# Summing the expert rows into the residual during the expert phase of a cross-attention and mixture-of-experts layer

## The chip, the cores and the metric

The kernel runs as one program on one core of a Trainium2 chip. The metric is the device time of one execution in microseconds (us); lower is better. An execution is somewhat longer than the span of the profile, which goes from the first instruction to the last.

## What is computed

64 sequences of 128 tokens with 256 features pass through one layer in float32. Cut to what matters:

```python
ln = layernorm(x)                                  # 64 x 128 x 256
x  = x + cross_attention(ctx, ln, mask, ...)       # 4 heads of 64, keys from ctx and from x itself
h  = layernorm(x)
w, idx = route(h)                                  # 4 of 32 experts for each token, with weights
mixed  = sum over the 4 of  w * down_e( silu(gate_e(h)) * up_e(h) )
shared = shared_down( silu(shared_gate(h)) * shared_up(h) )
x  = x + mixed + shared
```

So the output row of a token is its residual row, plus four weighted rows from four experts, plus one row from the shared expert.

## The kernel before

The order of all work is written out by hand, with semaphores between the engines. A unit is two sequences (256 tokens); there are 32. A tile is 128 rows that all go to one expert; there are 287 (`TILES`). The program has three stages.

**Attention, 32 units.** For each unit the engines project, score, mix and route. The residual of all 64 sequences stays in SBUF (`x1`). `rows_to_scatter` (L1099) normalises the new residual, `turn_n1` (L742) turns it on TensorE so that the features lie on the partitions, and `n1_copy` (ACT, L1188) copies the turned rows into the tile `n1T`, from which the router's logits are computed. For the first `EARLY` = 8 units SyncE also saves `n1T` to the DRAM tensor `n1T_kept` (`save_n1T`, L407), and `n1_copy` of the next unit waits until that has landed. For all units VectorE keeps the mean and the scale of each row in `mr` (L1446, L1447), at the end of the chain that makes them. GpSimd scatters four copies of each normalised row into the DRAM tensor `lists`, sorted by expert (`scatter_row`, L556); SyncE makes the copies (`spread_rows`, L401) and blanks the pages (L389). SyncE's queue is in order: what waits there holds back all behind it.

At the end of this stage the shared expert of the first 8 units is computed (`shared_up` L916, `shared_down` L927), while the last rows are still scattered, from turned rows that `load_n1T` (L417) has loaded back.

**Expert phase, 287 tiles.** SyncE loads tile t (`load_tile`, L466) into one of 8 slots (`xs`, parts of `pay`), as soon as TensorE has turned tile t - 8. In its iteration t TensorE projects tile t (L1033), turns tile t + 2 (L1024), and multiplies tile t - 1 by its expert's down weights (L1043). ACT evicts and applies silu (L1315, L1320, L1326). VectorE's iteration t is, in this order: `hidden(t)` (L1865), `keep_dest(t + 4)` (L1878), which reads the last two columns of tile t + 4, and `weigh_result(t - 1)` (L1872). GpSimd scatters the weighted rows into the DRAM tensor `expert_out` (L701), where the four rows of a token lie side by side. The rows of unit u can be in any tile up to tile 39 + 8u, and in no later one.

**Last stage, units 8 to 31.** After the last tile, ACT normalises the residual of a unit again from `mr` (`norm_again`, L1272), TensorE turns it (`shared_turn`, L895), ACT copies it to SBUF (`turned`, L1279), and TensorE computes the shared expert (L916, L927). VectorE multiplies (L1747), adds the shared result to `x1` (L1755), and sums the four expert rows of a unit (`sum_experts`, L1895 and L1897) and the residual (`sum_all`, L1903; `sum_last`, L1910) into `res`. SyncE loads the four rows of a unit (`load_er`, L484, 1 MB) and stores the sums (`store`, L488; the last unit in two halves, L498). Because the first 8 units have no shared work left, 32 units are summed within the time of 24.

## Time and profile before

| | us |
|---|---|
| median of 3 runs | 1342.62 |
| lowest and highest | 1340.92, 1345.98 |
| the profiled execution's own time | 1343.46 |
| its span | 1341.5 |
| attention stage, with the early shared work, in the span | 0 to about 742 |
| expert phase | about 742 to 1193 |
| last stage | 1193 to 1341.5 |

The profile's tables name an engine, a line of the kernel and the tiles written and read. PE is TensorE's matmul, PEld its weight load, DVE VectorE, ACT ScalarE, POOL GpSimd, SP SyncE with the queue SPq. A matmul in float32 shows as two records in the trace, so the 8 matmuls of a `shared_up` half (2 of the gate, 2 of the up weights, each two records) read as x8. The engines' busy shares of the span are TensorE 97%, ACT 75%, VectorE 72% and GpSimd 48%; they are means over three stages that have different limits.

### The profile page before, as it was taken

The numbers are of one execution on the slowest core, as the hardware profiler recorded it, in microseconds if no ns is written. First come the engines' busy times: TensorE is split into PE (matmuls) and PEld (weight loads), VectorE is DVE, ScalarE is ACT, GpSimd is POOL, SyncE is SP. The second block draws the span as 40 slices with busy tenths as digits, with TensorE's granted clock in tenths as the row PEclk, the third lists the DMA queues.
The fourth block names the chain that finished last, engine by engine and source line by source line (L and its number), as shares of the span: only waits on it lengthen the run. The fifth ranks groups of instructions, "written<-read, shape, count | busy, mean of one in ns | idle before, by whom it ended". The sixth has DMA issues, their size and how long they took to land.

```text
span 1341.5 us, 32944 instructions
## 1 busy us (share of the span) xinstructions
PE 1298.0 (97%) x8718; PEld 1043.2 (78%) x8718; DVE 972.0 (72%) x4498; ACT 1011.6 (75%) x2730; POOL 643.4 (48%) x724
## 2 busy tenths in 40 slices
PE   6999999999999999999979899999999999999997
PEld 4566676676676766766658799999999999988886
DVE  4578898888988988888887455555555555548887
ACT  4899999999999999999851566766776676653332
POOL 1113555555555555555455366666666666640000
PEclk8999999999999999999989899999999999999999
DMA  8234645535545445454487655555655555438896
GB/s 278 84 133 136 205 162 176 192 131 187 176 138 190 161 153 195 136 179 162 168 304 246 194 169 172 172 172 168 178 169 174 169 173 166 132 114 313 304 319 218
DMA packets 147714, 247.14 MB, mean 184 GB/s; under 512 B 24139, under 2 KB 110413, under 8 KB 146896
## 3 DMA queue, kind: packets, MB, share of 16 engines
q1 hardware_dynamic: 121472, 177.63, 41.3%
q0 software_dynamic: 26064, 67.42, 14.5%
q8 instruction: 77, 1.26, 0.4%
q14 instruction: 101, 0.83, 0.2%
HBM read 104.68 MB, written 119.96 MB: 167 GB/s over the span
## 4 chain that ended last, share of the span: by engine, by line
PE 63%; ACT 21%; DVE 9%; issue 5%; DMA 2%; SPq 0%; POOL 0%; ACTq 0%; DVEq 0%
PE psT L1033 10%; PE ps L1033 9%; PE psS L1043 9%; ACT arena L1168 6%; PE ps L916 6%; PE ps L1024 5%; PE ps L852 4%; ACT arena L1160 4%; PE psS L927 3%; PE psT L827 3%; PE psS L813 3%; PE psO L840 2%; ACT arena L1128 2%; ACT arena L1132 2%; ACT arena L1175 2%
## 5 line engine op out<-in xcount | busy, mean ns | idle before, releaser
L701 POOL DMA_INDIRECT expert_out<-pay,dest x287 | 282.1, 983 | 175.1 <-DVE dest L1878 157.4
L556 POOL DMA_INDIRECT lists<-pay,slot x168 | 174.3, 1037 | 187.7 <-PE psT L827 39.6
L1043 PE MATMUL psS<-arena,history 128*128 x574 | 171.8, 381 | 0.3 <-DVE history L1865 0.3
L1033 PEld LDWEIGHTS ps<-pad,hist_j 128*128 128x128 f32 x1152 | 152.1, 193 | 9.5 <-ACT pad L1315 2.1
L1033 PEld LDWEIGHTS psT<-pad 128*128 128x128 f32 x1144 | 151.0, 192 | 7.3
L1033 PE MATMUL ps<-pad,hist_j 128*128 128x128 f32 x1152 | 152.8, 276 | 1.9 <-ACT pad L1315 1.9
L1033 PE MATMUL psT<-pad 128*128 128x128 f32 x1144 | 151.6, 276 | 0.0
L1872 DVE TENSOR_SCALAR pay<-psS,dest 128x256 f32<-128x256 f32 x287 | 138.9, 484 | 1.6 <-PE psS L1043 1.5
L757 PE MATMUL ps<-arena 128*128 128x512 f32 x256 | 128.3, 624 | 2.6 <-ACT arena L1120 2.0
L556 POOL DMA_INDIRECT lists<-arena,slot x88 | 91.0, 1034 | 79.4 <-PE psT L827 20.6
L1168 ACT ACTIVATE arena<-arena,rden 128x256 f32<-128x256 f32 x256 | 109.1, 503 | 15.2 <-DVE rden L1466 15.1
L1865 DVE TENSOR_TENSOR history<-history,psT 128x128 f32<-128x128 f32 x143 | 41.2, 288 | 102.4 <-ACT history L1326 102.4
L1865 DVE TENSOR_TENSOR history<-history,ps 128x128 f32<-128x128 f32 x144 | 41.5, 288 | 101.2 <-ACT history L1326 101.2
L1024 PE MATMUL ps<-ident,pay 128*128 128x128 f32 x574 | 110.0, 274 | 3.1 <-DMA arena<-in_gate_up 3.0
L1315 ACT ACTIVATE pad<-ps 128x256 f32<-128x256 f32 x287 | 107.7, 375 | 0.0
L1320 ACT ACTIVATE hist_j<-arena 128x512 f32 x144 | 89.6, 622 | 9.4 <-issue 7.6
L1326 ACT ACTIVATE history<-ps 128x128 f32<-128x128 f32 x144 | 39.9, 277 | 70.3 <-PE ps L1033 70.3
L757 PEld LDWEIGHTS ps<-arena 128*128 128x128 f32 x256 | 44.2, 193 | 59.2 <-issue 59.2
L1320 ACT ACTIVATE pad<-arena 128x512 f32 x143 | 88.8, 621 | 0.0
L1326 ACT ACTIVATE history<-psT 128x128 f32<-128x128 f32 x143 | 39.7, 278 | 65.0 <-PE psT L1033 65.0
L1043 PEld LDWEIGHTS psS<-arena,history 128*128 128x128 f32 x574 | 86.9, 192 | 0.7 <-issue 0.7
L1418 DVE TENSOR_REDUCE va<-arena 128x12 f32<-128x768 f32 x64 | 61.0, 953 | 34.2 <-ACT arena L1128 29.1
(238 smaller groups left out, 3284.1 us busy)
## 6 DMA issues: line engine op xcount, KB each, us to landing
lists<-pad SPq DMA_DIRECT2D x72, 516.0 KB, 5.2
pay<-lists SPq DMA_DIRECT2D x287, 129.0 KB, 2.2
arena<-expert_out SPq DMA_DIRECT2D x32, 1024.0 KB, 7.1
pay<-pay SPq DMA_DIRECT2D x42, 384.0 KB, 3.6
x<-in_x SPq DMA_DIRECT2D x32, 256.0 KB, 4.7
out<-arena SPq DMA_DIRECT2D x31, 256.0 KB, 5.8
arena<-arena SPq DMA_DIRECT2D x20, 384.0 KB, 3.4
arena<-in_ctx SPq DMA_DIRECT2D x32, 192.0 KB, 4.6
```

The lines of the kernel that those rows point to most:

```text
L556: pool.indirect_dma_start(lists, bass.IndirectOffsetOnAxis(ap=slots(u)[:, j, k:k + 1], axis=0), paid(u)[:, j, k, :], None).then_inc(scat[3 ...
L701: pool.indirect_dma_start(expert_out, bass.IndirectOffsetOnAxis(ap=dest[:, t % DESTS, 1:2], axis=0), yy[n], None, bounds_check=T * TOPK - ...
L757: m = pe.matmul(ps[0][:, :], lnT[:, k, tok], w_lat[:, k, 0:2 * D], start=k == 0, stop=k == 1)
L916: m = pe.matmul(up_banks[u % 2][mm][:, which * D:(which + 1) * D], w[:, k, mm * P:(mm + 1) * P], n1T_of(u)[:, k, :], start=k == 0, stop=k ...
L1024: m = pe.transpose(ps[n % 2][:, k * P:(k + 1) * P], xs[n][:, k * P:(k + 1) * P], ident[:, :])
L1033: m = pe.matmul(ps[2 + n % 2][:, which * P:(which + 1) * P], w_now[1 - n % 2][:, k, which * I:(which + 1) * I], xsT[:, n % 2, k * P:(k + 1 ...
L1043: pe.matmul(dbank[n % 2][:, 0:D], hh[:, n % 4, :], w_dn[:, at(e, 1), :].rearrange("p a n -> p (a n)"), start=True, stop=True)\
L1168: a = act.activation(probs[:, j, g, :], probs[:, j, g, :], ACT.Copy, scale=rden[:, j, g:g + 1])
L1315: act.activation(xsT[:, n % 2, :], ps[n % 2][:, 0:D], ACT.Copy).then_inc(xst_ev, 1)
L1320: act.activation(w_now[1 - n % 2], w_gu[:, at(e, 1)].rearrange("p a k n -> p (a k) n"), ACT.Copy)\
L1865: dve.tensor_tensor(hh[:, n % 4, :], sg[:, n % 4, :], ps[2 + n % 2][:, P:2 * P], ALU.mult)\
L1872: dve.tensor_scalar(yy[n], dbank[n % 2][:, 0:D], dest[:, t % DESTS, 0:1].bitcast(fp32), None, ALU.mult)\
```

## The change

Five things are changed together.

1. The four expert rows of units 0 to 28 (`IN_PHASE` = 29) are summed into `x1` in the expert phase. SyncE loads them in pieces of two rows for each token of one sequence (`load_piece`, 256 KB, 116 pieces) into a new tile `side` with room for 3 pieces, one piece after every second tile from tile 55 on. Each piece waits until the piece three before it has been added. The first piece of unit u also waits until all tiles up to 39 + 8u are scattered. VectorE adds one row of a piece (`add_row`, 128 x 256) at the end of each of its iterations 53 to 284, 232 in all.
2. Units 0 to 7 are stored to the output in the expert phase, the others in the last stage, straight from `x1`. `res` and `sum_all` are gone. Units 29, 30 and 31 are still summed in the last stage, from loads of 1 MB.
3. The turned rows of all 32 units are saved to `n1T_kept`, and `n1_copy` waits for the save before it at every unit.
4. `norm_again`, `shared_turn`, `turned` and `mr` are gone. The last stage loads the turned rows of units 8 to 31 from DRAM: unit 8 into `side`, the others into a ring of four (`n1T_ring`).
5. TensorE waits, ahead of the last stage, for the last tile's turned rows and hidden rows, no longer for the last weighted result; that wait is now ahead of the first `shared_down` of the stage.

The masks and the bias of the output projection now share SBUF with `side`, since they are last read before the first piece arrives.

```diff
+PIECES = 3
+IN_PHASE = 29
+PIECE_LOAD, PIECE_ADD = 55, 53
+N1T_RING = 4
...
-                if (s + -2).exists() and s.n - 2 < EARLY:
+                if (s + -2).exists():
                     save_n1T(s + -2)
...
             spread_rows(Unit(UNITS // 2 - 1, 0))
-
+            save_n1T(Unit(UNITS // 2 - 1, 0))
...
+            def load_piece(q):
+                u, b, half = q // 4, q // 2, q % 2
+                if q % 4 == 0:
+                    for n in range(SLOTS):
+                        sp.wait_ge(y_out[n], 16 * (E // SLOTS + 1 + u))
+                ge(sp, summed, 2 * (q - PIECES + 1))
+                sp.dma_start(side[:, q % PIECES, :].rearrange("p (k n) -> p k n", k=2), er_d[:, b, 2 * half:2 * half + 2, :])\
+                  .then_inc(piece_in[q % PIECES], 16)
...
             for t in range(TILES):
                 load_tile(t, t % SLOTS)
...
+                q, odd = divmod(t - PIECE_LOAD, 2)
+                if odd == 0 and 0 <= q < 4 * IN_PHASE:
+                    load_piece(q)
+                done, odd = divmod(t - PIECE_LOAD - 17, 8)
+                if odd == 0 and 0 <= done < EARLY:
+                    sp.wait_ge(summed, 8 * (done + 1))
+                    store(done)
...
+            sp.wait_ge(summed, 2 * 4 * IN_PHASE)
+            sp.dma_start(side[:, 0, :], n1T_kept[EARLY]).then_inc(first_n1T_in, 16)
+            sp.wait_ge(w_ready, TILES)
+            for u in range(EARLY + 1, EARLY + 1 + N1T_RING):
+                load_late_n1T(u)
             for n in range(SLOTS):
                 sp.wait_ge(y_out[n], 16 * ((TILES - 1 - n) // SLOTS + 1))
...
+            for u in range(EARLY, UNITS - 1):
+                sp.wait_ge(sx_done, 2 * u + 2)
+                if u + N1T_RING + 1 < UNITS:
+                    load_late_n1T(u + N1T_RING + 1)
+                store(u)
...
-            pe.wait_ge(yy_done, TILES)
-            shared_turn(EARLY)
+            pe.wait_ge(xst_ev, TILES)
+            pe.wait_ge(hh_done, TILES)
             for u in range(EARLY, UNITS + 1):
                 if u < UNITS:
                     shared_up(u, 0)
-                if u + 1 < UNITS:
-                    shared_turn(u + 1)
-                if u < UNITS:
                     shared_up(u, 1)
                 if u >= EARLY + 1:
                     shared_down(u - 1)
...
-                ge(act, n1T_saved, 16 * upto(u.n, EARLY))
+                ge(act, n1T_saved, 16 * u.n)
...
-                    dve.scalar_tensor_tensor(mr[:, at(2 * u.n, 2), 0], mv[:, 4:6, 0], -1.0, ra[:, 4:6], ALU.mult, ALU.mult)
-                    dve.tensor_copy(mr[:, at(2 * u.n, 2), 1:2], ra[:, 4:6].rearrange("p (j o) -> p j o", o=1))
...
+            def add_row(q, k):
+                dve.wait_ge(piece_in[q % PIECES], 16 * (q // PIECES + 1))
+                ge(dve, summed, 2 * q + k)
+                xb = x1[:, q // 2, :]
+                dve.tensor_tensor(xb, xb, side[:, q % PIECES, k * D:(k + 1) * D], ALU.add).then_inc(summed, 1)
...
                 if t >= 1:
                     weigh_result(t - 1, (t - 1) % SLOTS)
+                if 0 <= t - PIECE_ADD < 2 * 4 * IN_PHASE:
+                    add_row((t - PIECE_ADD) // 2, (t - PIECE_ADD) % 2)
```

Three places show how the order moves. The changed kernel has other line numbers: its L1859, L1872, L1866 are L1865, L1878, L1872 before; its L469 is L466; its L936 and L949 are L916 and L927.

VectorE in the expert phase, two tiles, before (`history` holds the hidden rows, `pay` the tile slots and results, `dest` the kept columns):

```order
L1865 TENSOR_TENSOR history<-history,ps 128x128
L1878 COPY dest<-pay 128x2
L1872 TENSOR_SCALAR pay<-psS,dest 128x256
L1865 TENSOR_TENSOR history<-history,psT 128x128
L1878 COPY dest<-pay 128x2
L1872 TENSOR_SCALAR pay<-psS,dest 128x256
```

The same two tiles after the change:

```order
L1859 TENSOR_TENSOR history<-history,ps 128x128
L1872 COPY dest<-pay 128x2
L1866 TENSOR_SCALAR pay<-psS,dest 128x256
L1879 TENSOR_TENSOR x<-x,side 128x256
L1859 TENSOR_TENSOR history<-history,psT 128x128
L1872 COPY dest<-pay 128x2
L1866 TENSOR_SCALAR pay<-psS,dest 128x256
L1879 TENSOR_TENSOR x<-x,side 128x256
```

One add stands behind each weighted result, and ahead of the next tile's hidden rows.

SyncE's queue in the expert phase, with what each transfer waits for; before, the tile loads stand alone between the last weights and the loads of the last stage:

```order
L466 DMA pay<-lists 128x258 x6
L466 DMA pay<-lists 128x258 [waits dest_kept,xst_full] x279
L484 DMA arena<-expert_out 128x2x1024 [waits y_out5,y_out4,y_out6,y_out3,y_out7,y_out2,dn_full,y_out1,y_out0]
L484 DMA arena<-expert_out 128x2x1024 x3
L484 DMA arena<-expert_out 128x2x1024 [waits dC]
```

After the change, one unit's share of the queue:

```order
L481 DMA side<-expert_out 128x512 [waits y_out5,y_out4,y_out6,y_out3,y_out7,y_out2,summed,y_out1,y_out0]
L469 DMA pay<-lists 128x258 [waits dest_kept,xst_full]
L485 DMA out<-x 128x2x256 [waits summed]
L469 DMA pay<-lists 128x258 [waits dest_kept,xst_full]
L481 DMA side<-expert_out 128x512 [waits summed]
L469 DMA pay<-lists 128x258 [waits dest_kept,xst_full] x2
L481 DMA side<-expert_out 128x512 [waits summed]
```

Every second tile load now stands behind a piece that waits for VectorE's adds (`summed`).

TensorE in the last stage, one unit and the start of the next, before:

```order
L916 MATMUL ps<-arena,w_sg 128x256 x2
L916 MATMUL ps<-arena,w_su 128x256 x2
L895 MATMUL psO<-ident,arena 128x128 x4
L916 MATMUL ps<-arena,w_sg 128x256 x2
L916 MATMUL ps<-arena,w_su 128x256 x2
L927 MATMUL psS<-w_sd,arena 128x256 x4
L916 MATMUL psT<-arena,w_sg 128x256 x2
```

After:

```order
L936 MATMUL ps<-arena,w_sg 128x256 x2
L936 MATMUL ps<-arena,w_su 128x256 x2
L936 MATMUL ps<-arena,w_sg 128x256 x2
L936 MATMUL ps<-arena,w_su 128x256 x2
L949 MATMUL psS<-w_sd,arena 128x256 x4
L936 MATMUL psT<-arena,w_sg 128x256 x2
```

The four transposes between the halves of a unit are gone; the rest keeps its order.

## Rows read from the trace of the kernel before

**Rows 1.** Windows: PE, PEld, DVE, ACT, POOL busy us; granted clock; DMA share; GB/s.
```profile
760.00:1190.00 430.00, 430.00 (x3345) 415.68 (x3344) 231.69 (x835) 299.83 (x837) 273.61 (x280) 1.00 0.56 163
1196.00:1200.00 4.00, 4.00 (x14) 3.19 (x14) 0.30 (x1) 1.11 (x3) 0.16 (x1) 0.57 0.34 76
1204.00:1330.00 126.00, 126.00 (x628) 111.00 (x627) 105.35 (x177) 48.61 (x110) 0.00 (x0) 1.00 0.89 311
```

**Rows 2.** Chain that ended last, one unit of the last stage (start, us, what).
```profile
1303.81 1.73 PE psT L916 x8
1305.54 0.44 PE psO L895 x4
...
1307.70 1.73 PE psS L927 x8
1309.43 1.73 PE ps L916 x8
```

**Rows 3.** The same chain, early shared work of the first units.
```profile
718.22 3.45 PE ps L916 x16
...
723.40 1.73 PE psT L916 x8
```

**Rows 4.** Timeline of TensorE at the head of the last stage.
```profile
1192.52 0.69 PE L1043 MATMUL psS<-arena,history 128*128 x2 [0.35 <-DVE history L1865]
...
1195.81 1.74 PE L916 MATMUL ps<-arena,w_sg 128*128 128x256 f32 x4 [0.69 <-ACT arena L1279]
...
1202.40 1.13 PE L916 MATMUL psT<-arena,w_sg 128*128 128x256 f32 x4 [0.75 <-ACT arena L1279]
```

**Rows 5.** Timeline of VectorE, two iterations before the end of the expert phase.
```profile
1189.56 0.48 DVE L1872 TENSOR_SCALAR pay<-psS,dest 128x256 f32<-128x256 f32 x1
```

**Rows 6.** DMA issues: size of each, median us from issue to landing.
```profile
pay<-lists SPq DMA_DIRECT2D x287, 129.0 KB, 2.2
out<-arena SPq DMA_DIRECT2D x31, 256.0 KB, 5.8
n1T_kept<-arena SPq DMA_DIRECT2D x8, 256.0 KB, 5.0
arena<-in_gate_up SPq DMA_DIRECT2D x1, 256.0 KB, 2.8
```

**Rows 7.** Timeline at the end of the program.
```profile
1329.58 1.89 PE L927 MATMUL psS<-w_sd,arena 128*128 128x256 f32 x8
...
1338.36 0.75 DVE L1910 TENSOR_TENSOR arena<-arena,x 128x256 f32<-128x256 f32 x2
```

**Rows 8.** Timeline of one tile in the middle of the expert phase.
```profile
961.32 0.98 POOL L701 DMA_INDIRECT expert_out<-pay,dest  x1 [0.56 <-DVE dest L1878]
...
962.06 0.60 PE L1043 MATMUL psS<-arena,history 128*128 x2
...
962.35 0.29 DVE L1865 TENSOR_TENSOR history<-history,psT 128x128 f32<-128x128 f32 x1 [0.71 <-ACT history L1326]
```

**Rows 9.** Timeline in the attention stage, VectorE and GpSimd side by side.
```profile
458.56 1.83 DVE L1454 TENSOR_TENSOR arena<-arena,ra 128x768 f32<-128x768 f32 x2
...
459.76 1.46 POOL L556 DMA_INDIRECT lists<-arena,slot  x1 [2.20 <-PE psT L827]
```

**Rows 10.** Timeline of GpSimd behind the last tile.
```profile
1195.18 0.98 POOL L701 DMA_INDIRECT expert_out<-pay,dest  x1 [0.30 <-issue]
```

**Rows 11.** Chain that ended last, the same step of attention in units 6 and 16 apart.
```profile
108.33 1.09 PE psT L827 x8
...
231.91 1.09 PE psT L827 x8
...
561.30 1.09 PE psT L827 x8
```

**Rows 12.** Timeline at the end of attention: SyncE's last copies, ACT's last turned rows.
```profile
691.62 1.29 SPq L401 DMA_DIRECT2D pay<-pay  x2
...
698.75 0.60 ACT L1188 ACTIVATE arena<-psO 128x512 f32<-128x512 f32 x1 [0.75 <-PE psO L742]
```

More of the change, by code:

```diff
@@ L342, in wide @@
             return v.rearrange("(a n) -> a n", a=1).to_broadcast([P, v.shape[0]])
-        er = arena[:, 0:ER_DEPTH * 2 * TOPK * D].rearrange("p (a j k n) -> p a j k n", a=ER_DEPTH, j=2, k=TOPK)
-        used[0] = ER_DEPTH * 2 * TOPK * D
+        er = arena[:, 0:(UNITS - IN_PHASE) * 2 * TOPK * D].rearrange("p (a j k n) -> p a j k n", a=UNITS - IN_PHASE, j=2, k=TOPK)
+        used[0] = (UNITS - IN_PHASE) * 2 * TOPK * D
         esum, e2 = part(2, D), part(2, 2, D)
-        res = part(2, 2, D)
-        late_set = [part(2 * D) for _ in range(4)]
+        late_set = [part(2 * D) for _ in range(2)]
+        n1T_ring = [part(2 * D) for _ in range(N1T_RING)]
+        assert used[0] <= E * 2 * D
         first_n1T, above, below_wo = 6, 6 + EARLY, 17
@@ L466, in load_tile, with store @@
                 sp.dma_start(xs[n], lists[at(t * P, P), :]).then_inc(xs_in[n], 16)
+            er_d = expert_out.rearrange("(b p k) n -> p b k n", p=P, k=TOPK)
+            out_d = out.rearrange("b p n -> p b n")
+            def load_piece(q):
[6 more added lines that the diff above has]
+                  .then_inc(piece_in[q % PIECES], 16)
+            def store(u):
+                sp.dma_start(out_d[:, 2 * u:2 * u + 2, :], x1[:, 2 * u:2 * u + 2, :]).then_inc(stored, 16)
+            sp.wait_ge(mask_ready, UNITS)
+            sp.wait_ge(biased, UNITS)
+            sp.wait_ge(s_full, NB)
             for t in range(TILES):
@@ L490, in _ @@
-            for v in range(ER_DEPTH):
-                load_er(v)
-            for v in range(UNITS - 1):
-                if v + ER_DEPTH < UNITS:
-                    load_er(v + ER_DEPTH)
-                store(v)
+            for v in range(IN_PHASE, UNITS):
+                sp.dma_start(er[:, v - IN_PHASE], er_d[:, 2 * v:2 * v + 2]).then_inc(er_in[v - IN_PHASE], 16)
+            for u in range(EARLY, UNITS - 1):
[3 more added lines that the diff above has]
+                store(u)
@@ L923, in shared_down @@
                     pe.wait_ge(pt_ev, NB - 1)
+                if u == EARLY:
+                    pe.wait_ge(yy_done, TILES)
                 for j in range(2):
@@ L1265, in _ @@
             in_order(step, UNITS)
-            def norm_again(u):
-                ge(act, nt_full, u - EARLY)
-                for j in range(2):
-                    b = 2 * u + j
-                    a = act.activation(n1_of(u)[:, j, :], x1[:, b, :], ACT.Identity,
-                                       bias=mr[:, b, 0:1], scale=mr[:, b, 1:2])
-                a.then_inc(nh, 1)
-            def turned(u):
-                act.wait_ge(nt_full, u - EARLY + 1)
-                ge(act, sgu_full, 2 * u)
-                act.activation(n1T_of(u).rearrange("p k n -> p (k n)"), psO[:, :], ACT.Copy).then_inc(nt_ev, 1)
             def shared_silu(u, mm):
@@ L1918, in _ @@
                     add_shared(u - 1)
[L1919 to L1923 removed]
+                if u % 3 == 1 and u // 3 - 5 in range(UNITS - IN_PHASE):
+                    sum_experts(IN_PHASE + u // 3 - 5)
+            dve.wait_ge(er_done, UNITS - IN_PHASE)
             add_shared(UNITS - 1)
[L1925 to L1926 removed]
 def kernel(x, ctx_768, mask_BxS2_bk0, L0_xattn_ln_x_g, L0_xattn_ln_x_b, L0_xattn_ln_l_g, L0_xattn_ln_l_b,
```

105 lines of the change are left out of this document (35 added, 70 removed).

## The prediction

> **What bounds the kernel now.** I read the windows of the span first, to see which stage has room, then the chain that ended last in each stage, then the timelines where stages meet, and the DMA issues last. In the expert phase TensorE is busy in all of the window at a granted clock of 1.00, while VectorE is busy 231.69 of 430 us, and the DMA engines 0.56 [rows 1]. In the body of the last stage TensorE is again busy throughout, and the DMA engines are at 0.89 with 311 GB/s, near the end of their range. So both stages are TensorE's, and a change gains only where it takes TensorE's work, or a gap of TensorE, away.
>
> The chain of the last stage has TensorE alone in it: a half of the shared up-projection 1.73 us, four transposes 0.44, the other half, the down-projection 1.73. Unit to unit it is 1309.43 - 1303.81 = 5.62 us [rows 2]. The early shared work has the same matmuls without the transposes, from loaded turned rows: 723.40 - 718.22 = 5.18 us a unit [rows 3]. This is what the changed last stage should look like, on the same chip in the same execution.
>
> **The change part by part, against the profiled execution (span 1341.5, own time 1343.46).**
>
> *Body of the last stage.* From the start of unit 9's up-projection on, 22 turns (units 10 to 31) are removed: 22 x 0.44 = 9.7 us [rows 2]. VectorE loses three large sums for each of 32 units, and has only hidden rows and shared adds left, with three units' sums among them; ACT loses three evictions a unit. Both were faster than TensorE there, so this gives nothing by itself. SyncE's loads fall from 32 MB to about 9 MB. A load of turned rows is issued when unit u's shared result is added, for unit u + 5, some three units (15 us) ahead of its use; a 256 KB transfer behind a 1 MB one took 5.8 us in the worst such company [rows 6]. It is covered.
>
> *Head of the last stage.* TensorE's last matmul of the tiles ends at 1192.52 + 0.69 = 1193.21. Then come the last weighted result, a normalisation, a turn and a copy, and the first up-projection starts at 1195.81, and unit 9's at 1202.40 [rows 4]: 9.2 us for what is 2 x 1.73 of matmuls. Behind the idle stretch the granted clock was 0.57, that is partly the lower of its two levels (1.2 instead of 2.4 GHz) [rows 1], and the first four matmul records took 1.74 us for 0.86. After the change unit 8's turned rows are loaded when the last add is done, in iteration 284: the weighted result of that iteration starts at 1189.56 [rows 5], the add ends some 0.8 us later, and a 256 KB load lands in 2.8 us [rows 6]: 1193.3. TensorE then idles for 0.1 to 0.5 us; I take 0.3. New head: 0.3 + 3.46 = 3.8 us, gain 5.4. Bounds: with a landing of 5.0 us [rows 6] the gap is 2.4 and the clock falls again, and the gain is 9.2 - 2.4 - 3.46 - 1.5 = 1.8 us; with no gap it is 5.7.
>
> *Tail.* The down-projection of unit 30 starts at 1329.58, and the program ends at 1341.5, 11.9 us later; VectorE's sums and a wait for a store lie between. The last add ends at 1338.36 + 0.75 = 1339.11, so the last store takes 2.4 us [rows 7]. After the change: two down-projections (3.46), one shared add of 0.42 with its wait (0.5), the store (2.4): 6.4 us, gain 5.5. Nothing in it is unknown, so its bounds are 5 and 6.
>
> *Expert phase, VectorE.* 232 adds of 128 x 256 from two SBUF inputs. Two such took 0.75 us together [rows 7], so one is about 0.37. VectorE idles 0.71 us ahead of each hidden row, waiting for ACT [rows 8], and that is exactly where the add stands; 0.34 remains. If it were late: the hidden row ends at 962.64, and the down-projection that needs it starts one tile (1.545 us, which is 430 us over 278 tiles) after 962.06, at 963.60 [rows 8]: another 0.96 us of slack. Cost 0. If both covers were gone, all 232 x 0.37 = 86 us would show, an end far from these rows.
>
> *Expert phase, GpSimd.* Its scatter takes 0.98 us, and the smallest gap between two was 0.30 [rows 8, 10]: a pitch of 1.28 for 1.545. In attention a scatter that began while VectorE ran an operation with two SBUF inputs took 1.46 us instead, and the VectorE operation was not longer [rows 9]. The add is of this kind. So a scatter may take up to 0.37 more: a pitch of 1.65, 0.1 over the tile. But then the scatter slides later against the add, meets less of it, and settles at the tile's pace; results have 8 slots. I take 0, the nearest end; the other is 232 x 0.1 = 23 us. The Trainium skill (SBUF — State Buffer, Who interferes with whom) says that a VectorE operation with two SBUF inputs contends with a GpSimd operation that reads SBUF, but infers that descriptor generation needs the other interface and is spared. By that inference the scatters would stay at 0.98 and this term is 0 for certain; the row of 1.46 speaks against it, and the sum is the same by both.
>
> *Expert phase, SyncE.* The piece that goes out after tile 55 + 2q waits for VectorE's iteration 48 + 2q, and tile 56 + 2q is behind it. VectorE needs that tile's last columns in iteration 52 + 2q. That is four iterations (6.2 us) less the 0.95 or so between the place of those columns in an iteration and its end: 5.2 us, of which 0.5 goes for the two issues. The tile load may take 4.7 us. It took 2.2 [rows 6]; with 256 KB ahead of it, at 311 GB/s [rows 1] 0.8 us, I take 3.0 to 3.4. The upper bound is 5.8, the stores behind 1 MB at a share of 0.89 [rows 6]. The new traffic is 116 pieces and 8 stores, 32 MB in 360 us or 90 GB/s, which at the last stage's rate (311 / 0.89) is 0.26 of the engines: 0.56 becomes 0.82. I take the lower, since a burst is 0.5 MB, not 1.3. Cost 0; what a miss costs is a rival.
>
> *Attention.* 24 more saves of 256 KB, each in SyncE's queue ahead of the next unit's loads, and a wait on ACT. Units with saves (to unit 7) took (231.91 - 108.33) / 6 = 20.60 us, those without (561.30 - 231.91) / 16 = 20.59 [rows 11]: nothing. Two small VectorE operations a unit leave, off the chain. The one tight place is the end: the save of unit 30 is issued at about 692.9, behind two copies, and ACT's last turned rows want it at 698.75 [rows 12], 5.8 us for a median of 5.0 [rows 6]. 0 to 2 us, and 0 is nearer.
>
> Sum: 9.7 + 5.4 + 5.5 = 20.6 us, less 0.4 for what the small margins may cost: the span becomes 1321.3, the execution (2.0 more) 1323.3. The profiled execution was 0.8 above the median, so the time is **1322 us**.
>
> **Rivals.**
>
> *The tile loads come late (slower).* The wait on the adds cuts SyncE's lead from eight tiles to about five. If a tile load takes L, four iterations cannot be shorter than 0.95 + 0.5 + L. It costs from L = 4.7 on, and at L = 5.1 a tile is 0.09 us longer, 232 of which eat the 20.6 us. At 5.8 a tile takes 1.81 and the program 20.6 - 61 = 41 us more than before: about 1383. For it: one in-order queue, and a share of 0.82. Against: 2.2 us now. Chance 0.08.
>
> *GpSimd becomes the pace.* If every scatter met a whole add in spite of sliding, 23 us would be lost and the time is about 1345, no change. The rows of 1.46 are for it, the sliding against. The same rule of the Trainium skill says that whichever of the two starts first holds the port and the other waits for all of it. As a mechanism here: an add that meets a running scatter waits up to 0.7 us, till 962.30, and the hidden row starts 0.3 late, inside its 0.96 of slack; the time would be 1322 again. With both, no change: chance 0.07.
>
> *A part of the gain is lost.* The head gets 1.8 instead of 5.4, or bursts on the full DMA engines cost half a microsecond in every tenth tile, or the last save stalls ACT by 2: 1326 to 1334. Chance 0.1.
>
> **How the numbers follow.** The forecast (1318 to 1326) has 0.75. A measurement can tell 0.5%, 6.7 us, from no change. Faster by more than that: the forecast and nearly all of the partial case, 0.84; the same: 0.08; slower: 0.08. The range reaches from 1317, where no gap and no stall is left, into the partial case at 1331.
>
> **What would show it.** Right: TensorE's chain of the last stage with 5.18 us a unit and no psO group; the first up-projection within 0.5 us of the last tile's down-projection, at full clock; the program's end some 6.4 us after unit 30's down-projection starts; the pitch of 1.545 us a tile unchanged, with VectorE's idle time ahead of the hidden row halved. Wrong: waits of VectorE on `pay<-lists` or on `side<-expert_out` in the expert phase; scatters of over 1.2 us with TensorE waiting on `yy_done`; a window of the expert phase in which TensorE is not at its full busy time; an ACT wait on `n1T_kept`.

## The result, and the profile after

| | before | after |
|---|---|---|
| median of the runs beside each other, us | 1343.59 (4 runs) | 1324.42 (4 runs) |
| lowest and highest | 1340.92, 1345.98 | 1321.65, 1327.15 |
| ratio, 95% interval | | 0.9858, 0.9829 to 0.9887 |
| the profiled execution's own time | 1343.46 | 1323.8 |
| its span | 1341.5 | 1321.7 |

The change takes 19 us off, 1.4%. The forecast was 1322 us in a range of 1317 to 1331. The profiled span is 19.8 us shorter, and three stretches make it up. Lines of the changed kernel: `shared_up` is L936, `shared_down` L949, the down-projection of the tiles L1065, the scatter L728, the new add L1879, the last columns' copy L1872.

Windows of the changed kernel, columns as in [rows 1]:

```profile
760.00:1190.00 430.00, 429.87 (x3343) 415.30 (x3341) 307.26 (x1065) 299.31 (x835) 319.62 (x278) 1.00 0.78 239
1200.00:1315.00 115.00, 115.00 (x534) 101.26 (x533) 44.77 (x98) 17.24 (x45) 0.00 (x0) 1.00 0.39 122
```

In the expert phase VectorE has 76 us more than in [rows 1], the DMA engines went from 0.56 to 0.78 (0.82 from 860 us on, where the pieces run), and TensorE is still busy throughout. In the last stage the DMA engines fell from 0.89 to 0.39. What the change moved out of the last stage found room in the phase ahead of it.

The chain that ended last, in the last stage:

```profile
1237.96 1.73 PE psS L949 x8
1239.68 1.73 PE psT L936 x8
1241.41 1.73 PE ps L936 x8
1243.14 1.73 PE psS L949 x8
```

From one down-projection to the next it is 5.18 us, with no group of turns between the halves, where [rows 2] had 5.62.

Timeline of TensorE at the head of the last stage, and of the last work at its end:

```profile
1193.82 0.69 PE L1065 MATMUL psS<-arena,history 128*128 x2 [0.35 <-DVE history L1859]
1194.55 1.10 PE L936 MATMUL ps<-side,w_sg 128*128 128x256 f32 x4
...
1198.08 1.03 PE L936 MATMUL psT<-arena,w_sg 128*128 128x256 f32 x4
...
1315.49 3.62 PE L949 MATMUL psS<-w_sd,arena 128*128 128x256 f32 x16
...
1318.80 1.14 SPq L526 DMA_DIRECT2D out<-x  x2
1319.15 0.42 DVE L1749 TENSOR_TENSOR x<-x,psS 128x256 f32<-128x256 f32 x1 [0.37 <-PE psS L949]
```

The tiles end at 1194.51 and the first up-projection starts 0.04 us later, without the slower records behind an idle stretch (1.10 us for four, where [rows 4] had 1.74). Head, from the end of the tiles to the start of unit 9's up-projection: 1198.08 - 1194.51 = 3.57 us in place of 9.19. Body, from there to the start of unit 30's down-projection: 117.41 in place of 127.18. Tail, from there to the end of the program: 6.21 in place of 11.92. That is 5.62 + 9.77 + 5.71 = 21.1 us. The other 1.3 us were given back ahead of the last stage: 0.5 in the expert phase, about 0.8 before its second tile. The experiments take these apart.

**GpSimd and VectorE in the expert phase.** Two tiles of the same execution, from the timeline:

```profile
846.04 0.16 DVE L1872 COPY dest<-pay 128x2 int32<-128x2 int32 x1
...
846.35 0.98 POOL L728 DMA_INDIRECT expert_out<-pay,dest  x1 [0.56 <-DVE dest L1872]
846.58 0.42 DVE L1879 TENSOR_TENSOR x<-x,side 128x256 f32<-128x256 f32 x1
...
956.67 0.41 DVE L1879 TENSOR_TENSOR x<-x,side 128x256 f32<-128x256 f32 x1
956.70 1.24 POOL L728 DMA_INDIRECT expert_out<-pay,dest  x1 [0.30 <-DVE dest L1872]
...
957.47 0.29 DVE L1859 TENSOR_TENSOR history<-history,psT 128x128 f32<-128x128 f32 x1 [0.38 <-issue]
957.67 0.27 DVE L1872 COPY dest<-pay 128x2 int32<-128x2 int32 x1
```

At 846 the scatter starts 0.23 us ahead of the add, and neither is longer than alone. At 956 it starts 0.03 us behind the add's start and takes 1.24 us in place of 0.98. Its smallest gap, 0.30, is left in front of it, and 1.24 + 0.30 = 1.54 us is the pace of the tiles. The idle time ahead of the hidden row is 0.38, where [rows 8] had 0.71.

### The profile page after: what moved, and what is told of

Read it like the earlier page. It is cut to its first block, busy times and chain, and to the rows that moved or that the text cites. A ratio compares the mean times of both kernels' runs of the same rounds, so it can differ in the third digit from the quotient of the medians.

```text
span 1321.7 us, 33188 instructions
## 1 busy us (share of the span) xinstructions
PE 1286.8 (97%) x8622; PEld 1034.2 (78%) x8622; DVE 979.1 (74%) x4578; ACT 976.4 (74%) x2658; POOL 687.8 (52%) x724
## 3 DMA queue, kind: packets, MB, share of 16 engines
q8 instruction: 76, 1.25, 0.4%
## 4 chain that ended last, share of the span: by engine, by line
PE 65%; ACT 21%; DVE 8%; issue 5%; DMA 1%; ACTq 0%; SPq 0%; POOL 0%; DVEq 0%
PE ps L1055 10%; PE psT L1055 10%; PE psS L1065 9%; PE ps L936 6%; ACT arena L1187 6%; PE ps L1046 5%; PE psS L949 4%; PE ps L879 4%; ACT arena L1179 4%; PE psT L854 3%; PE psS L840 3%; PE psO L867 2%; ACT arena L1147 2%; ACT arena L1151 2%; ACT arena L1194 2%
## 5 line engine op out<-in xcount | busy, mean ns | idle before, releaser
L728 POOL DMA_INDIRECT expert_out<-pay,dest x287 | 329.8, 1149 | 129.5 <-DVE dest L1872 115.1
L1065 PE MATMUL psS<-arena,history 128*128 x574 | 172.2, 382 | 0.5 <-DVE history L1859 0.3
L1866 DVE TENSOR_SCALAR pay<-psS,dest 128x256 f32<-128x256 f32 x287 | 138.9, 484 | 1.4 <-PE psS L1065 1.3
L1879 DVE TENSOR_TENSOR x<-x,side 128x256 f32<-128x256 f32 x232 | 96.4, 416 | 0.0
L573 POOL TENSOR_TENSOR x<-x,side 128x512 f32<-128x512 f32 x32 | 40.7, 1272 | 93.7 <-PE psS L845 93.7
L1065 PEld LDWEIGHTS psS<-arena,history 128*128 128x128 f32 x574 | 86.9, 192 | 1.2 <-issue 1.1
L1859 DVE TENSOR_TENSOR history<-history,psT 128x128 f32<-128x128 f32 x143 | 41.2, 288 | 62.9 <-ACT history L1331 45.7
L1859 DVE TENSOR_TENSOR history<-history,ps 128x128 f32<-128x128 f32 x144 | 41.5, 288 | 62.2 <-ACT history L1331 60.6
```

The lines of the kernel that those rows point to most:

```text
L728: pool.indirect_dma_start(expert_out, bass.IndirectOffsetOnAxis(ap=dest[:, t % DESTS, 1:2], axis=0), yy[n], None, bounds_check=T * TOPK - ...
L1065: pe.matmul(dbank[n % 2][:, 0:D], hh[:, n % 4, :], w_dn[:, at(e, 1), :].rearrange("p a n -> p (a n)"), start=True, stop=True)\
L1859: dve.tensor_tensor(hh[:, n % 4, :], sg[:, n % 4, :], ps[2 + n % 2][:, P:2 * P], ALU.mult)\
L1866: dve.tensor_scalar(yy[n], dbank[n % 2][:, 0:D], dest[:, t % DESTS, 0:1].bitcast(fp32), None, ALU.mult)\
L1879: dve.tensor_tensor(xb, xb, side[:, q % PIECES, k * D:(k + 1) * D], ALU.add).then_inc(summed, 1)
```

## The experiments

The three groups of runs came from three chips. On those of the first and the third the kernel before took 1344.6 and 1345.4 us (9 runs each); on that of the second, called the second chip below, 1400.2 (23 runs). Times are compared inside a group only. To compare the expert phase alone I take from each profiled execution the stretch from the start of the tiles' second down-projection to the end of the last. It has 286 tiles, and leaves out what varies ahead of it. Scatters are counted as long when they take over 1.05 us, among all that touch the window of 860 to 1190 us. The third group's base is the changed kernel once more: 1323.55 us (5 runs, 1321.98 to 1325.93), where 1324 to 1325 had been expected, a ratio to before of 0.984.

### The base again

Edit: none.

> The changed kernel once more, beside the others of this group on the same chip, as their base. Every theory expects 1324 us within 2, scatters of 1.24 us from the adds on, and a tile load that lands late near 932 us of its profiled span.

1325.14 us (1321.78 to 1328.1), ratio to before 0.9849. The expert phase as defined above took 439.82 us; before 439.50, the first profile of the changed kernel 440.03. But only 112 of its 214 scatters were long, where the first profile had 186 of 214, with identical code. The late tile load stood at 934 us, and cost 0.3. The stage's second down-projection started at 756.56, and in the first profile at 754.48 (before: 753.71): the work ahead of the tiles differs by 2 us and more between executions of one kernel. So the 0.8 us given back there can't be put down to the change.

### SyncE's old lead

```diff
-IN_PHASE = 29
-PIECE_LOAD, PIECE_ADD = 55, 53
+IN_PHASE = 28
+PIECE_LOAD, PIECE_ADD = 59, 53
```

> The piece loads go out four tiles later, so that SyncE keeps about its old lead of eight tiles; unit 28 moves back into the last stage, whose sums are under TensorE's work. Theory (the half microsecond lost near 932 us is a tile load behind a burst of stores and a piece, and the lead covers it): no wait of VectorE on the tiles' pay rows in the expert phase, its windows at TensorE's full busy time, 0.5 us less than the changed kernel, 1323.9 for 1324.4. Rival (the loss has another cause): the same loss stands at the same place and the time is equal. If the new iterations' room does not cover the head, the gap ahead of the last stage grows from 0.04 us by up to 2.

1324.35 us, in the same group as 1325.14 for the base: the intervals of the ratios (0.9826 to 0.9869, 0.9825 to 0.9874) lie on each other. In the trace VectorE has no wait for a tile load between 760 and 1190 us, where the changed kernel had 3.4 us of them, and the expert phase took 439.51 us, as before the change. The second number alone is weak: of five executions with the tight lead, three took 439.80 to 440.03, but those of the third group's base and of its dummy turns took 439.51 too. What the loss is, where there is one, can be seen in the changed kernel's timeline, on SyncE's queue and on VectorE:

```profile
939.04 0.62 SPq L485 DMA_DIRECT2D out<-x  x1
939.76 3.13 SPq L469 DMA_DIRECT2D pay<-lists  x1
942.95 0.45 SPq L481 DMA_DIRECT2D side<-expert_out  x1
...
946.54 0.17 DVE L1872 COPY dest<-pay 128x2 int32<-128x2 int32 x1 [0.80 <-DMA pay<-lists]
```

Behind a piece, a tile load and a store, the issue of one load took 3.13 us in place of 0.4, all later issues slid, and TensorE's next two tiles took 1.92 and 1.64 us. An issue of over 2 us came once in this execution; issues of over 1 us came 12 times between 760 and 1190 us, and never in the kernel before. In this kernel there was room for nearly all of them: the half microsecond is in this trace, and too small for these medians.

### The add twice

```diff
+                dve.tensor_tensor(psO[:, 0:D], xb, side[:, q % PIECES, k * D:(k + 1) * D], ALU.add)
                 dve.tensor_tensor(xb, xb, side[:, q % PIECES, k * D:(k + 1) * D], ALU.add).then_inc(summed, 1)
```

> Each of the 232 iterations with an add has a second one of the same two SBUF inputs, whose result goes to an unused PSUM bank; what is computed does not change. VectorE had 0.38 us of idle time ahead of the hidden row and about 0.96 of slack behind it, and the second add takes 0.41: Theory (a scatter is only delayed where it starts while an add runs, and a scatter that falls behind slides to a place where it meets less of it, so that it settles at the tile's pace): a tile of 1.545 to 1.58, 0 to 8 us more than the changed kernel. Rival (each scatter pays for all the adds it meets): a scatter of 1.24 + 0.26 to 1.24 + 0.41, a pitch of 1.80 to 1.95, so 232 x 0.25 to 232 x 0.41 = 58 to 95 us more, about 1382 to 1419.

1324.06 us, 1.1 under the base. 98 us more of VectorE's work cost nothing; the expert phase took 439.80 us. The same stretch as the window of 760 to 1190, group by group, in this kernel:

```profile
L728 POOL DMA_INDIRECT expert_out<-pay,dest x279 | 288.6, 1034 | 142.3 <-DVE dest L1872 115.9 <-DVE pay L1866 9.0 <-issue 8.6
...
L1879 DVE TENSOR_TENSOR psO<-x,side 128x256 f32<-128x256 f32 x231 | 97.8, 424 | 0.0
L1880 DVE TENSOR_TENSOR x<-x,side 128x256 f32<-128x256 f32 x231 | 96.6, 418 | 0.0
```

And two scatters of it beside their adds, from the timeline:

```profile
951.29 0.42 DVE L1879 TENSOR_TENSOR psO<-x,side 128x256 f32<-128x256 f32 x1
951.62 0.42 DVE L1880 TENSOR_TENSOR x<-x,side 128x256 f32<-128x256 f32 x1
...
951.32 1.24 POOL L728 DMA_INDIRECT expert_out<-pay,dest  x1 [0.30 <-DVE dest L1872]
952.86 1.24 POOL L728 DMA_INDIRECT expert_out<-pay,dest  x1 [0.30 <-DVE dest L1872]
```

The scatter is no longer with two adds than with one: 1.24, never over 1.25, in all kernels of this group. Only 57 of 215 were long here; most of the others start 0.2 us ahead of the first add, meet both, and take 0.98. The rival (each scatter pays for all it meets, 58 to 95 us) has fallen. A scatter that has slid back lies in the tile where its delay is 0.26, and that is what is left between 1.28 and the tile's pace. What sets the delay is when it starts. Over the nine profiled executions with whole adds from loaded pieces, a scatter that starts from 0.03 us on behind the start of an add takes 0.98 + 0.30 us less that distance: 1.24 at 0.04, 1.11 to 1.15 at 0.15, 1.05 to 1.09 at 0.2, and 0.98 to 0.99 from 0.3 on. Starting earlier it is not longer.

### The add cut to a column, and the pieces with it

```diff
-                dve.tensor_tensor(xb, xb, side[:, q % PIECES, k * D:(k + 1) * D], ALU.add).then_inc(summed, 1)
+                dve.tensor_tensor(xb[:, 0:1], xb[:, 0:1], side[:, q % PIECES, k * D:k * D + 1], ALU.add).then_inc(summed, 1)
```

> The adds of the expert phase are cut to one column, so the sums of 255 columns of units 0 to 28 are left out; the piece loads, stores and waits stay. It tells what the adds cost in the expert phase, beside everything that comes with them. Theory (nothing on the path, they only lengthen the scatters to the tile's pace): the time of the changed kernel within 0.5 us, scatters of 0.98 us again, idle time of 0.7 ahead of the hidden row, and the late tile load near 932 us still there. Rival (the 1.3 us given back ahead of the last stage come from the adds): 1 us or more faster than the changed kernel. A third: if the scatter stays at 1.24, it is the fuller DMA queues and not the adds that lengthen it.

1324.96 us: the base again, and no rival. All scatters counted as above (215) are within 0.99 us, so it is the add that lengthens them, and not the fuller queues. The expert phase took 439.51 us. VectorE's waits for tile loads came to 0.8 us in the window of 760 to 1190, where the three profiles of the changed kernel had 3.4, 2.9 and 2.6: the late load that I had expected to stay is mostly gone. A short add ends sooner, and SyncE waits for it; that this is the reason was not tested.

In the third group the piece loads were cut as well:

```diff
-                sp.dma_start(side[:, q % PIECES, :].rearrange("p (k n) -> p k n", k=2), er_d[:, b, 2 * half:2 * half + 2, :])\
+                sp.dma_start(side[:, q % PIECES, :].rearrange("p (k n) -> p k n", k=2)[:, :, 0:1], er_d[:, b, 2 * half:2 * half + 2, 0:1])\
```

> The adds and the piece loads of the expert phase are both cut to one column (two of 128 x 1 in a piece), so the sums of 255 columns of units 0 to 28 are left out and 30 MB of traffic with them; waits and issues stay. Theory on a chip like the first (traffic and adds are both under cover): within 0.5 us of the changed kernel. On a chip like the second, where the expert phase took 507 us with pieces (507.9 with the second input in PSUM, 507.1 with the add) and 496 without them: 10 us or more faster than the changed kernel if it is the traffic that costs there, 0 to 2 us if it is the order of issues on SyncE.

1324.03 us beside 1323.55 for that group's base. The DMA share of the phase (752 to 1190 us) is 0.59 in place of 0.76, and the time is the same. On the chips of the first and the third group the whole of the moved sums, traffic and adds, costs nothing that can be measured. The waits and issues on SyncE stayed in both runs; what they can cost the next one shows.

### The pieces one step tighter

```diff
-                ge(sp, summed, 2 * (q - PIECES + 1))
+                ge(sp, summed, 2 * (q - PIECES + 2))
```

> A piece load waits for the add two iterations later than in the changed kernel: SyncE's lead over VectorE falls from four iterations to two, and the tile load behind it has to land in that. By the formula of the prediction two iterations are then at least 0.95 + 0.5 + L, with L the tile load's time, 3.0 to 3.4 us: 4.45 to 4.85 us for two tiles, 2.2 to 2.4 for one in place of 1.54, over 232 tiles 160 to 205 us more than the changed kernel. Rival (the formula's L is the median of a quiet queue, 2.2): 1.83 a tile and 66 us more. If the wait is not the limit at all: 0.

1471.38 us, 147.8 over the group's base. The waits from 760 to 1300 us:

```profile
DVE dest L1872 <- DMA pay<-lists: 228.4, 123, 4.0
POOL expert_out L728 <- DVE dest L1872: 193.1, 126, 15.7
```

The window from 850 to 1300, and the DMA issue of the tile loads (860 to 1300) with its landing time:

```profile
850.00:1300.00 450.00, 362.53 (x2472) 317.79 (x2472) 222.85 (x823) 223.48 (x619) 203.34 (x206) 0.98 0.58 185
```

```profile
pay<-lists SPq DMA_DIRECT2D x201, 129.0 KB, 3.0
```

The formula gives (0.95 + 0.5 + 3.0) / 2 = 2.23 us a tile. The window's 450 us hold 206 scatters, one a tile, which is 2.18 us. The pace came out just under the expected 2.2 to 2.4, and the 160 us or more were missed by 12, as (2.18 - 1.545) x 232 = 147 says. So the rival that I had given 0.08 was a real edge with the right formula: the changed kernel stands at a lead of four iterations and 4.7 us of room, with loads of about 3 (measured in this kernel, at a DMA share of 0.58); at a lead of two it costs 148 us. The half microsecond above is where a load of over 4.7 us came once.

### Dummy turns

```diff
                     shared_up(u, 0)
+                    for j in range(4):
+                        pe.transpose(psO[:, j * P:(j + 1) * P], ident[:, :], ident[:, :])
                     shared_up(u, 1)
```

> The changed kernel with the work of a turn put back on TensorE alone: four transposes of the identity into an unused PSUM bank between the halves of each up-projection of the last stage, 24 times. Nothing else of the old stage comes back (no eviction, no normalised rows, no large sums, no loads). Theory (the body's gain is TensorE's own time): 24 x 0.44 = 10.6 us more than the changed kernel, 1335, a unit of 5.62 us. Rival (the gain came from the DMA engines at 0.89 or from VectorE's sums): 0 to 3 us more, 1324 to 1327.

1402.04 us, on the second chip, where the changed kernel was not run: nothing can be said from that time alone. Again in the third group:

> The dummy turns again, because the group before this one had no run of the changed kernel on its chip. Theory (the body's gain is TensorE's own time): 24 x 0.44 = 10.6 us over the changed kernel of this group, within 1.5. Rival (the DMA engines or VectorE): 0 to 3 us.

1332.48 us beside 1323.55, so 8.9 us, a little under the bound of 9.1 that I had set; the profiled spans are 1331.4 and 1320.7, 10.7 us apart. The chain of the last stage:

```profile
1235.45 1.73 PE psS L949 x8
1237.18 1.73 PE ps L936 x8
1238.91 0.44 PE psO L1096 x4
1239.35 1.73 PE ps L936 x8
1241.07 1.73 PE psS L949 x8
```

A unit is 5.62 us again, with the DMA share of its window (1205 to 1320) at 0.32. The body took 127.51 us, where ten profiles without the dummy turns, on every chip used, have 117.41; with the head's 0.4 this is the 10.5 that the turns should cost. The medians differ by less because of what varies ahead of the last stage. With none of the old stage's loads, evictions or sums the old pace is back. The body's gain is TensorE's own time, and the rival (0 to 3 us) has fallen.

### The first turned rows late

```diff
             sp.wait_ge(summed, 2 * 4 * IN_PHASE)
+            for n in range(SLOTS):
+                sp.wait_ge(y_out[n], 16 * ((TILES - 1 - n) // SLOTS + 1))
             sp.dma_start(side[:, 0, :], n1T_kept[EARLY]).then_inc(first_n1T_in, 16)
...
-            for n in range(SLOTS):
-                sp.wait_ge(y_out[n], 16 * ((TILES - 1 - n) // SLOTS + 1))
```

> The changed kernel with the loads of the first turned rows of the last stage moved behind SyncE's waits for the last scattered rows. Theory (the head gains because these rows are there when the tiles end): TensorE waits some 8.5 us ahead of the first up-projection, and its granted clock falls behind that, 1.5 us more: 10 us more than the changed kernel, 1334. Rival (the wait overlaps with something that bounds the stage anyway): 3 us or less.

1402.57 us on the second chip, without a base beside it; the trace has the two terms apart:

```profile
1266.51 0.69 PE L1065 MATMUL psS<-arena,history 128*128 x2 [0.35 <-issue]
1274.52 2.04 PE L936 MATMUL ps<-side,w_sg 128*128 128x256 f32 x4 [7.32 <-DMA side<-n1T_kept]
1276.36 1.91 PE L936 MATMUL ps<-side,w_su 128*128 128x256 f32 x4
1278.06 1.49 PE L936 MATMUL ps<-side,w_sg 128*128 128x256 f32 x4
1279.39 1.03 PE L936 MATMUL ps<-side,w_su 128*128 128x256 f32 x4
1280.25 1.03 PE L936 MATMUL psT<-arena,w_sg 128*128 128x256 f32 x4
```

7.32 us of waiting, and then groups of four matmul records at 2.04, 1.91 and 1.49 us before they are at 1.03 again: the granted clock is 0.50 from 1274.5 to 1278, the lower level (1.2 GHz in place of 2.4), and 1.00 from 1280 on. This costs 5.73 - 3.53 = 2.2 us against the head of the changed kernel. Head: 1280.25 - 1267.20 = 13.05 us in place of 3.57 (3.58 in the last experiment, on this chip), 9.5 more; 10 were expected. The head's gain is that these rows are there when the tiles end.

### The turned rows without the sums' move

Into the kernel before (its large sums and their 32 loads of 1 MB stay in the last stage):

```diff
-n1T_kept = nc.dram_tensor("n1T_kept", [EARLY, P, 2 * D], fp32).ap()
+n1T_kept = nc.dram_tensor("n1T_kept", [UNITS, P, 2 * D], fp32).ap()
...
-                    pe.wait_ge(nt_ev, u - EARLY + 1)
+                    pe.wait_ge(late_n1T_in[(u - EARLY) % N1T_RING], 16 * ((u - EARLY) // N1T_RING + 1))
...
+            def load_late_n1T(u):
+                ge(sp, sgu_full, 2 * (u - N1T_RING + 1) if u >= EARLY + N1T_RING else 0)
+                sp.dma_start(n1T_ring[(u - EARLY) % N1T_RING], n1T_kept[u])\
+                  .then_inc(late_n1T_in[(u - EARLY) % N1T_RING], 16)
...
             for v in range(UNITS - 1):
                 if v + ER_DEPTH < UNITS:
                     load_er(v + ER_DEPTH)
+                while loaded_late < UNITS and loaded_late <= EARLY + N1T_RING - 1 + v * 3 // 4:
+                    load_late_n1T(loaded_late)
+                    loaded_late += 1
                 store(v)
...
-            pe.wait_ge(yy_done, TILES)
-            shared_turn(EARLY)
+            pe.wait_ge(xst_ev, TILES)
+            pe.wait_ge(hh_done, TILES)
```

> The kernel before with one half of the change: the turned rows of all units are saved and loaded from a ring of four, while all expert sums, with their 32 loads of 1 MB, stay in the last stage. Its DMA traffic is then 32 MB of expert rows, 8 MB of stores and 6 MB of turned rows, 48.3 million bytes. Theory (without the move of the sums the DMA engines take TensorE's place as the bound): at 311 / 0.89 = 350 GB/s these take 138 us, where TensorE wants 127; the gain over the kernel before is 2 to 8 us, 1336 to 1342, the DMA share in the body is over 0.95 and TensorE has gaps. Rival (the turned rows are the whole of the gain and the sums need not move): a unit of 5.18 us and 12 us or more off, 1332 or less.

1425.81 us beside 1400.19: slower by 1.65% (1.44 to 1.85), where I had expected 2 to 8 us less: neither the theory nor the rival. TensorE has gaps, but the DMA engines aren't full: their share, which was to be over 0.95 in the body, is 0.84 to 0.92 there and 0.80 over the stage. Waits from 1254 us on:

```profile
PE ps L920 <- DMA arena<-n1T_kept: 14.7, 5, 6.3
PE psT L920 <- DMA arena<-n1T_kept: 8.9, 5, 2.6
```

and two windows:

```profile
1280.00:1310.00 30.00, 25.41 (x98) 21.41 (x99) 19.32 (x32) 3.07 (x8) 0.00 (x0) 0.83 0.86 312
1340.00:1370.00 30.00, 23.72 (x99) 19.69 (x100) 22.47 (x36) 3.07 (x8) 0.00 (x0) 0.94 0.92 319
```

The matmuls wait 23.6 us for turned rows, and the clock falls behind the gaps. The chain that ended last says why the rows are late:

```profile
1272.88 1.15 DVE arena L1873
1274.04 0.36 SPq L493
...
1274.44 7.71 DMA arena<-n1T_kept
...
1282.20 5.99 PE ps L920 x16
```

L1873 is a unit's large sum of expert rows, which frees the buffer that L493, the next load of 1 MB, waits for. The load of turned rows stands behind that load in the queue, so it can't be issued before VectorE has come that far. TensorE was through with what it had at about 1276, and its place in the ring had been free since the up-projection of unit 8, which ended near 1258. The same links (sum, issue, a load of 5.5 to 7.8 us, TensorE) come seven times in the chain. So two things are mixed in this run: the large loads make a load of turned rows long, and this queue order issues it too late to cover even that. With the rows issued as soon as the ring is free the wait might be gone; that was not run. The stage took 168.6 us (1254.7 to the end), 283 GB/s on the mean, where my 138 had taken the 350 GB/s of full engines for the whole stage. With no base trace of that chip how much of the 168.6 is the chip's stays open. What holds is that there, with the large loads in the stage and in this order, loading the turned rows costs more than turning them. Whether the sums must move for the turned rows to pay is not shown.

### A second input from PSUM

```diff
-                dve.tensor_tensor(xb, xb, side[:, q % PIECES, k * D:(k + 1) * D], ALU.add).then_inc(summed, 1)
+                dve.tensor_tensor(xb, xb, psO[:, 0:D], ALU.add).then_inc(summed, 1)
```

> The add of the expert phase takes its second input from a PSUM bank instead of the loaded piece, so the sums of units 0 to 28 are left out; length, place and waits stay. Theory (only an operation with two SBUF inputs delays a scatter): scatters of 0.98 us throughout, as with the add cut to one column, and the last columns' copy at 0.16; behind a hiccup of the tiles GpSimd is back at its idle time of 0.56 within a few tiles. Rival (any operation of that length at that place does it): stretches with scatters of 1.24 us at a pitch of 1.54. The time is that of the changed kernel in both.

One run, 1394.25 us on the second chip, where the changed kernel was not run, so the time has no base. The scatter's group from 860 to 1250 us, here, and in the dummy-turns run of the same chip, whose adds have both inputs in SBUF:

```profile
L728 POOL DMA_INDIRECT expert_out<-pay,dest x217 | 213.5, 984 | 177.6 <-DVE dest L1872 132.6 <-issue 31.1 <-DVE pay L1866 6.9
```

```profile
L728 POOL DMA_INDIRECT expert_out<-pay,dest x217 | 220.8, 1018 | 170.8 <-DVE dest L1874 121.6 <-issue 35.2 <-DVE pay L1868 8.8
```

None of 182 scatters was long with one SBUF input, and 53 of 183 with two. The starts are alike in both (54 and 53 of them lie 0.1 to 0.2 us behind an add's start): beside one SBUF input these took 0.98 to 0.99 us, beside two 1.05 to 1.13. It is the second SBUF input that delays them.

The copy of the last columns, expected at 0.16, was a miss: 97 of 182 took over 0.2 us. The reason is in the other traces too. A copy that starts while a scatter has 0.2 to 0.4 us left ends about with it (0.27 us on the mean with 0.3 left, 0.36 with 0.4, over all profiles), and takes 0.16 with 0.6 to 0.9 us left or with none beside it. That goes by where it lies and not by how long the scatter is.

### The second chip

There TensorE doesn't bound the expert phase. The kernel before was timed there but not profiled, so the turned rows alone, whose expert phase has no pieces and no adds, stand in for it. Windows from 860 to 1250 us, of the dummy-turns run (with the pieces and adds) and of the turned rows alone (without them):

```profile
860.00:1250.00 390.00, 353.13 (x2595) 322.72 (x2595) 245.51 (x868) 228.33 (x651) 219.46 (x217) 1.00 0.71 219
```

```profile
860.00:1250.00 390.00, 365.77 (x2675) 334.61 (x2674) 179.44 (x668) 232.63 (x669) 219.51 (x224) 0.99 0.48 142
```

A tile took 1.80 and 1.74 us, with TensorE busy 0.91 and 0.94, at full clock. The timeline (here of the dummy turns, ACT alone) has a pause in each third tile, from the start of the phase on; the turned rows alone have it too:

```profile
829.15 0.28 ACT L1333 ACTIVATE history<-ps 128x128 f32<-128x128 f32 x1 [1.75 <-PE ps L1055]
829.32 0.62 ACT L1327 ACTIVATE hist_j<-arena 128x512 f32 x1
```

The expert phase took 507.1 us (dummy turns), 506.9 (late rows) and 507.9 (input from PSUM), against 495.8 with no adds and no pieces (the turned rows alone). So 11 to 12 us of the change's gain go there. As the input from PSUM had scatters of 0.98 and the same 508, it isn't the length of the scatters; whether it is the adds' time on VectorE, the traffic or the waits on SyncE was not tried on that chip. What makes the pause of 1.75 us isn't in the records and stays open. The last stage is the same on that chip (body 117.41 us, tail 6.21). Taking their known 9 to 11 us off the dummy turns and 9.5 off the late rows puts the changed kernel at 1391 to 1393 us there, and the run with the input from PSUM took 1394: a gain of 6 to 9 in place of 19 to 22. This is an inference, as the changed kernel was not run on that chip.

## Why the prediction was right

- **Body, 9.7 us.** 9.77 in the trace; the dummy turns gave the old pace back with TensorE's work alone (127.51 for 117.41).
- **Head, 5.4, bounds 1.8 to 5.7.** 5.62: the gap was 0.04 us in place of 0.3, and 0.0 to 0.5 in the other kernels of the first and third groups. Late rows cost 9.5 us, of which the lower clock is 2.2; the 1.5 of the lower bound was too small for a wait as long as that one.
- **Tail, 5.5.** 5.71.
- **VectorE, 0.** The add took 0.415 us and not 0.37, a tenth too small; two adds in one record can't be halved for the price of one, since they overlap (in the doubled kernel they start 0.33 apart). The first add left 0.38 of idle time, and a second one fitted into that, since it adds only 0.33. The slack of 0.96 behind the hidden row was not drawn on, so whether it is real was not tested.
- **GpSimd, 0.** Where a scatter was delayed it slid and settled at the tile's pace, as argued, with 0.26 in place of up to 0.37. What I had not seen is that it need not get there: where it starts ahead of the add it is not lengthened at all, and most changes from the one place to the other stand beside a late load or a longer gap between scatters (186 of 214, 112 of 214 and 94 of 215 long in three executions of one kernel). The Trainium skill (SBUF — State Buffer, Who interferes with whom) infers that descriptor generation is spared by such an add. The runs show that the scatter as a whole is not: 1.24 for 0.98 with two SBUF inputs, 0.98 with one; which part of it waits they don't show. Its rule that the later of the two waits for all of the earlier doesn't hold for whole instructions: an add of 0.42 us that began 0.23 into a scatter was not longer, and a scatter that began 0.03 into an add paid 0.26 of the 0.38 that was left of it. As the delay falls by as much as the scatter starts later and is gone at 0.3, the rule may still hold for a short part at the scatter's start; no run decides that.
- **SyncE, 0, and the rival at 0.08.** The landing of 3.0 us under the tighter wait is the lower end of what I took. In the profiled execution two tiles came late behind the one long issue, 0.5 us in all; the partial case had named losses of this size, but in every tenth tile. The share forecast for the time of the pieces, 0.82, was met (860 to 1190 us).
- **Attention, 0.** The save of unit 30 was issued at 694.07, and ACT did not wait for it. The 0.8 us given back ahead of the second tile are less than the 2 us by which executions of one kernel differ there.
- The 0.4 us for small margins was too little for that one profile (1.3), and the gains of head, body and tail, 0.5 above the forecast together, made up a part of it: 1321.7 for a forecast span of 1321.3. That the two errors nearly cancel is luck of half a microsecond, far inside the range.

No term of the sum failed. The forecast rests on the chip, though: the cover for the adds and pieces was read from one chip's trace, and on the second some 11 us of it were not there. What was wrong was an expectation behind the prediction (the turned rows alone: a loss of 25.6 us for a gain of 2 to 8). It made the DMA engines the bound, and they were busy 0.80 of the stage; the chain there goes through the place of the loads in SyncE's queue. The same arithmetic in the prediction (issued some three units ahead of its use) is what keeps the changed kernel's body at 117.41.

## What to carry to other kernels

Work that is moved under another stage's bound is free as long as that stage has the cover for it (on the second chip some 11 us were missing) and the in-order queue that feeds it keeps its lead: price the lead (iterations times pace, less the place of the use and the issues) against the landing time, since one step too few cost 148 us here and the exact formula was at hand. A small, urgent load has the same price behind large ones in one queue: the turned rows behind the sums' loads of 1 MB were issued too late and took 5.5 to 7.8 us to land, and the kernel lost 25.6 us, though the DMA engines were busy only 0.80 of the stage. Ask for each such load what the queue waits for ahead of it. And when an engine is delayed by a neighbour, ask whether it can slide: with slack in the pace, doubling the disturbance cost nothing here.

## What the hardware showed that I had not expected

- The delay of a scatter by an add with two SBUF inputs depends on when it starts (0.23 us ahead: none; 0.03 behind: 0.26; from there on 0.30 less the distance; none from 0.3 on), so one kernel has two patterns and changes between them in an execution, without a change in its time.
- The copy of two columns (L1872) takes 0.27 to 0.36 us in place of 0.16 where it starts 0.3 to 0.4 us ahead of the end of a running scatter, long or short; with 0.6 to 0.9 us left it takes 0.16.
- The issue of a 129 KB load took 3.13 us once on SyncE, behind a piece, a tile load and a store, in place of some 0.4. Issues of over 1 us came with the pieces (none of 271 between 760 and 1190 us before, 12 of 395 after), and stayed with the pieces cut to a column (16 of 396), so the bytes alone don't make them. The turned rows alone, on the second chip and without pieces, had four.
- One program took 1344 us on one chip and 1400 on another. By the kernels that were profiled there the difference of 56 us is in the expert phase (495.8 for 439.5 us without adds, 1.74 us a tile for 1.54), with TensorE's granted clock at 0.99 to 1.00. A gain that rests on cover found on one chip can be partly uncovered on the other.
